# A new opening order, and twelve steps by halves in place of six, in a feature net in split fp32

## The chip, the cores and the metric

One core of a Trainium2 chip. The metric is the device time of the kernel in microseconds, the median of several runs. Engines: TensorE (PE in the profile; its weight loads are PEld), VectorE (DVE), ScalarE (ACT), GpSimd (POOL), SyncE (SP), which here issues nearly all loads.

## The reference

```python
# features (512, 2, 5128), W_ft (512, 5128), stm (512, 2, 1); r_features has 1024 rows of the batch
w = jnp.einsum('bpf,mf->bpm', features, W_ft) + b_ft
accumulator = stm * w
l1_x = jnp.clip(accumulator, 0.0, 1.0).reshape(features.shape[0], -1)
l2_x = jnp.clip(l1_x @ W1.T + b1, 0.0, 1.0)
return l2_x @ W2.T + b2
```

For a batch of 1024 and two perspectives nearly all of the work is one product in fp32: 512 outputs x 2048 columns over 5128 features. What follows (bias, scale by `stm`, clip, two small layers) is short.

## The kernel before

**The split.** A product in fp32 is made of three in fp32r: each operand is rounded to a `hi` part on ScalarE, VectorE takes the remainder `lo` = raw - `hi`, and TensorE adds `hi*hi`, `hi*lo` and `lo*hi`. The big product is also done by a two by two block scheme with seven block products in place of eight: features go in pairs of 128 rows (A, the first, and B, the second), outputs in two halves of 256 and columns in two halves of 1024. Three passes of 20 steps and a last one of 10 make `STEPS` = 70. A step takes one pair and adds two block products, a first half (`pos` 0) and a second (`pos` 1), each twelve products of 128x128 by 128x512: two row tiles by two column tiles by three splits.

**The steps of pass 0.** The first half of step g takes raw blocks as they are loaded: w block 0 and x block 0. I call it A of g. The second half needs sums: `sums_of(g)` on VectorE (lines 398 to 422) adds two w blocks (line 407, `w_sum`), subtracts two x blocks (line 417, `x_sum`) and keeps a further combination of w for later (line 421, `s_kept`). I call the second half B of g. So A needs loads, a rounding and a remainder; B needs loads, sums, a rounding and a remainder.

**Steps by halves and whole steps.** The first `OPEN` = 6 steps run by halves in the order `OPEN_HALVES`: A0 A1 B0 A2 B1 B2 A3 B3 A4 B4 A5 B5. ScalarE's `open_half` (290 to 315) rounds w, then x of one half, VectorE's `open_low` (380 to 396) takes their remainders (389 for w, 394 for x, 1024 columns), and TensorE's `open_products` (562 to 593) issues four `hi*hi`, four `lo` w by `hi` x, and four `hi` w by `lo` x, waiting for counts of `open_hi` and `open_lo` in turn. From step 6 on ScalarE's `round_step` (317) rounds both halves of w in one instruction (324) and of x in another (329, 2048 columns), VectorE's `low_step` (437) takes both remainders the same way (440, 443), and TensorE's `step` (595) waits once for each. The order on VectorE is written out by hand (476 to 492): in whole steps `sums_of(g + 1)` stands ahead of `low_step(g)`, and before the first of them `sums_of(6)` as well. At steps 13, 15, 16 and 17 VectorE also prepares the last eight feature rows (496, 502, 506).

**Buffers.** `HI` = 3 sets of rounded operands; a half of step g waits until step g - 3 is done (`step_done`, raised by the last product of B). `RAW` = 6 slots of raw blocks; the load of step g waits for step g - 6. The first `STAGED` = 3 steps load their A blocks to `open_x` and `open_w`, which lie in the room of `c_early`.

**Loads.** SP issues them in program order: w block 0 of step 0, its x block in two pieces of 512 columns, then for the halves of the staged steps in their order (221 to 228), then for steps 3 and on (229 to 252). A load of one x block is 512 KB, of one w block 128 KB; a whole step of pass 0 is 1.44 MB. ScalarE issues none. GpSimd waits for `step_done` 9 and then clears and loads the last rows' operands.

**Warm-up.** TensorE starts with `WARM_UP` = 16 products of 256 columns on zeros (680).

Of the kernel before, what the change touches and what calls it, by code (L numbers as in the profile page):

```python
# [24 lines left out]
ACT = mybir.ActivationFunctionType  # L25

P = 128
BANK = 512
WARM_UP = 16
K_PAIRS = 20  # L30
COLS = 1024
MH = 256
PASSES = 3
STEPS = PASSES * K_PAIRS + K_PAIRS // 2
STAGED = 3
OPEN = 6
RAW = 6
RAW_HOME = 4
HI = 3
OPEN_HALVES = ((0, 0), (1, 0), (0, 1), (2, 0), (1, 1), (2, 1), (3, 0), (3, 1), (4, 0), (4, 1), (5, 0), (5, 1))  # L40
TURN = 2 * K_PAIRS

HALVES = (((0, 0, 0), (1, 1, 4)), ((1, 1, 0), (0, 0, 4)), ((1, 0, 0), (0, 1, 4)), ((0, 0, 0), (1, 1, 0)))
# [7 lines left out]
def feature_net(nc, x_p, w_p, x_rest, w_rest, stm, b_ft, w1_t, b1, w2_t, b2, out):  # L51
# [10 lines left out]
    with ctx:  # L62
        base = (nc.sbuf_base + 63) // 64 * 64

        place = [base]
# [10 lines left out]
        def sem(name):  # L76
            return ctx.enter_context(nc.semaphore(name))
# [16 lines left out]
        c_at = place[0]  # L94
# [1 line left out]
        c_late = sb("c_late", [P, 2, 2 * COLS], at=xs_at + 4 * CST * COLS)  # L96
        c_all = [c_early[:, 0, :], c_early[:, 1, :], c_late[:, 0, :], c_late[:, 1, :]]
        open_x = sb("open_x", [P, STAGED, COLS], at=c_at)
        open_w = sb("open_w", [P, STAGED, MH], at=c_at + 4 * STAGED * COLS)
        xr_raw = sb("xr_raw", [P, COLS], at=c_at)  # L100
        wr_raw = sb("wr_raw", [P, 4, MH], at=c_at + 4 * COLS)
        xr = sb("xr", [P, COLS], F32R)
        wr = sb("wr", [P, 4, MH], F32R)

        stm_at = xs_at + 4 * (TST + 4) * COLS
# [20 lines left out]
        open_x_loaded = [sem(f"open_x_loaded{j}") for j in range(STAGED + 1)]  # L126
        open_hi = sem("open_hi")
        open_lo = sem("open_lo")
        x_sum = sem("x_sum")
        w_sum = sem("w_sum")  # L130
        s_kept = sem("s_kept")
# [83 lines left out]

        @block.sync
        def _(sp):
            sp.dma_start(open_w[:, 0, :], w_p[0, :, 0, :]).then_inc(open_w_loaded[0], 16)
            sp.dma_start(open_x[:, 0, 0:BANK], x_p[0, :, 0, 0:BANK]).then_inc(open_x_loaded[0], 16)
            sp.dma_start(open_x[:, 0, BANK:COLS], x_p[0, :, 0, BANK:COLS]).then_inc(open_x_loaded[STAGED], 16)  # L220
            for g, pos in OPEN_HALVES[1:2 * STAGED]:
                if pos == 0:
                    sp.dma_start(open_w[:, g, :], w_p[g, :, 0, :]).then_inc(open_w_loaded[g], 16)
                    sp.dma_start(open_x[:, g, :], x_p[g, :, 0, :]).then_inc(open_x_loaded[g], 16)
                else:
                    sp.dma_start(ws[:, raw_w(g) + 1, :], w_p[g, :, 1, :]).then_inc(w_loaded[g], 16)
                    sp.dma_start(ws[:, KEPT + g, :], w_p[g, :, 2, :]).then_inc(s_loaded[g], 16)
                    sp.dma_start(xs[:, TST + g, :], x_p[g, :, 1, :]).then_inc(t_loaded[g], 16)
            for g in range(STAGED, STEPS):
                f, k = pass_of(g)  # L230
                if g in (TURN + RAW_HOME, TURN + RAW_HOME + 1):
                    sp.wait_ge(x_sum, TURN + 2 * (g - TURN - RAW_HOME + 1))
                elif TURN <= g < TURN + RAW_HOME:
                    sp.wait_ge(step_done, g - RAW_HOME + 1)
                elif g >= RAW:
                    sp.wait_ge(step_done, g - RAW + 1)
                i, j, n = raw_w(g), raw_x(g), slot(g)
                if f == 0:
                    sp.dma_start(ws[:, i:i + 2, :], w_p[k, :, 0:2, :]).then_inc(w_loaded[n], 16)
                    sp.dma_start(ws[:, KEPT + k, :], w_p[k, :, 2, :]).then_inc(s_loaded[n], 16)  # L240
                    sp.dma_start(xs[:, j, :], x_p[k, :, 0, :]).then_inc(x_loaded[n], 16)
                    sp.dma_start(xs[:, TST + k, :], x_p[k, :, 1, :]).then_inc(t_loaded[n], 16)
                elif f == 1:
                    sp.dma_start(ws[:, i:i + 2, :], w_p[k, :, 0:2, :]).then_inc(w_loaded[n], 16)
                    sp.dma_start(xs[:, j:j + 2, :], x_p[k, :, 1:3, :]).then_inc(x_loaded[n], 16)
                elif f == 2:
                    sp.dma_start(ws[:, i:i + 2, :], w_p[k, :, 2:4, :]).then_inc(w_loaded[n], 16)
                    sp.dma_start(xs[:, j:j + 2, :], x_p[k, :, 2:4, :]).then_inc(x_loaded[n], 16)
                else:
                    for pos in range(2):  # L250
                        sp.dma_start(ws[:, i + pos, :], w_p[2 * k + pos, :, 3, :]).then_inc(w_loaded[n], 16)
                        sp.dma_start(xs[:, j + pos, :], x_p[2 * k + pos, :, 3, :]).then_inc(x_loaded[n], 16)
                if g == TURN + 10:
                    sp.wait_ge(x_sum, TURN + 6)
                    sp.dma_start(stm_all[:, :, :].rearrange("p h n -> p (h n)"),
                                 stm.rearrange("(a n) -> a n", a=1).broadcast_to([P, 2 * COLS]))\
                        .then_inc(stm_loaded, 16)
            for n, h in enumerate((1, 0)):
                sp.wait_ge(res_ready, n + 1)
                sp.dma_start(out.rearrange("(h q n) -> h q n", h=2, q=Q)[h], res[:, h, :]).then_inc(stored, 16)  # L260
            sp.wait_ge(stored, 32)
# [27 lines left out]
        def _(sc):  # L289
            def open_half(n, g, pos):  # L290
                if g >= HI:
                    sc.wait_ge(step_done, g - HI + 1)
                if pos == 0 and g < STAGED:
                    sc.wait_ge(open_w_loaded[g], 16)
                    nc.scalar.activation(w_hi[:, g, 0, :], open_w[:, g, :], ACT.Copy).then_inc(open_hi, 1)
                    sc.wait_ge(open_x_loaded[g], 16)
                    if g == 0:
                        nc.scalar.activation(x_hi[:, 0, 0, 0:BANK], open_x[:, 0, 0:BANK], ACT.Copy)\  # L298
# [2 lines left out]
                        nc.scalar.activation(x_hi[:, 0, 0, BANK:COLS], open_x[:, 0, BANK:COLS], ACT.Copy)\  # L301
                            .then_inc(open_hi, 1)
                    else:
                        nc.scalar.activation(x_hi[:, g, 0, :], open_x[:, g, :], ACT.Copy).then_inc(open_hi, 1)  # L304
                elif pos == 0:
                    sc.wait_ge(w_loaded[slot(g)], w_count(g))
                    nc.scalar.activation(w_hi[:, g % HI, 0, :], ws[:, raw_w(g), :], ACT.Copy).then_inc(open_hi, 1)
# [23 lines left out]
            def drain(f):  # L331
                for b in range(8):
# [16 lines left out]
                    else:  # L349
# [2 lines left out]
                        nc.scalar.activation(to, src, ACT.Identity, bias=b_ft_col[:, m:m + 1])\  # L352
                            .then_inc(drained, 1)

            for n, (g, pos) in enumerate(OPEN_HALVES):
                open_half(n, g, pos)
            for g in range(OPEN, STEPS):
# [21 lines left out]
        def _(dve):  # L379
# [93 lines left out]
                                        b2_col[:, 0:1], None, ALU.add).then_inc(res_ready, 1)  # L473

            nc.vector.memset(idle[:, :], 0.0).then_inc(idle_zeroed, 1)
            open_low(0, 0, 0)
            open_low(1, 1, 0)
            sums_of(0)
            open_low(2, 0, 1)
            open_low(3, 2, 0)  # L480
            sums_of(1)
            open_low(4, 1, 1)
            sums_of(2)
            open_low(5, 2, 1)
            for g in range(STAGED, OPEN):
                sums_of(g)
                open_low(2 * g, g, 0)
                open_low(2 * g + 1, g, 1)
            sums_of(OPEN)
            fourth = PASSES * K_PAIRS  # L490
            for g in range(OPEN, STEPS):
# [61 lines left out]
        def _(pe):  # L553
# [8 lines left out]
            def open_products(n, g, pos):  # L562
# [3 lines left out]
                if n == 0:  # L566
# [8 lines left out]
                    for c in range(PERSP):  # L575
                        pe.wait_ge(open_lo, 2 + c)
                        for m in range(2):
                            product(m * 2 + c, wh, xl, m, c, False)
                    return
                pe.wait_ge(open_hi, before + 2)  # L580
                for m in range(2):
# [7 lines left out]
                for m in range(2):  # L589
                    for c in range(PERSP):  # L590
                        mm = product(bank + m * 2 + c, wh, xl, m, c, False)
                if pos == 1:
                    mm.then_inc(step_done, 1)

            def step(g):
                f, k = pass_of(g)
# [156 lines left out]
```

## Time and profile before

| | |
|---|---|
| runs | 410.91, 411.74, 411.70 us, median 411.7 |
| the profiled execution | 409.96 us, its span 408.2 us |
| TensorE | 98% of the span busy, 1764 products |
| VectorE | 86%, 331 instructions |
| ScalarE | 47%, 182 instructions |
| HBM read | 96.08 MB, 235 GB/s over the span |

In the span's 40 slices TensorE is at nine tenths in nearly all, the first ones at 8, 9, 9, 9, 7; the transfer engines stand at 7, 9, 9, 9, 7 tenths there with 232, 400, 397, 399, 275 GB/s. The profile's times of products are modelled at their ends, so their pace is read from start to start. The views of use here are the timeline of the first 60 us, the chain of work that ended last, and the windows.

### The profile page before, as it was taken

The page shows a single profiled execution, that of the slowest core. Times are in us where ns is not written, and L with a number is a line of the kernel's source. Part 1 is how long each engine was busy: PE and PEld are TensorE (multiplying, and loading weights), DVE is VectorE, ACT ScalarE, POOL GpSimd, SP SyncE. Part 2 cuts the span into 40 slices and gives each one's busy share as a digit, 9 for nine tenths or more (in the row PEclk, how much of TensorE's full clock was granted, in tenths as well). Part 3 has the DMA queues.
Part 4 walks back from the last instruction along what each step waited for, and adds up shares of the span by engine and source line. Part 5 has one row for each costly group of instructions (what it writes and reads, how often), then busy time and mean ns, then how long its engine had stood idle before and what let it go on. Part 6 is the DMA issues. An engine that isn't in the chain of part 4 may idle for free.

```text
span 408.2 us, 4646 instructions
## 1 busy us (share of the span) xinstructions
PE 398.5 (98%) x1764; PEld 322.6 (79%) x1764; DVE 349.1 (86%) x331; ACT 191.4 (47%) x182; POOL 12.7 (3%) x32
## 2 busy tenths in 40 slices
PE   8999799999999999999999999999999999999995
PEld 5778688888888888888888888888888888888851
DVE  3999999899999999999984889999888755996335
ACT  4465644644474444444444854444444457444200
POOL 1000009000000000000000000000000000000000
PEclk9999999999999999999999999999999999999998
DMA  7999788987666777676506799876676777771000
GB/s 232 400 397 399 275 257 233 346 287 266 235 245 232 254 259 251 210 253 232 213 4 255 243 361 332 323 274 246 254 259 206 245 228 222 237 220 60 2 0 0
DMA packets 30182, 96.39 MB, mean 236 GB/s; under 512 B 3752, under 2 KB 9648, under 8 KB 24912
## 3 DMA queue, kind: packets, MB, share of 16 engines
q1 hardware_dynamic: 29536, 95.44, 67.7%
q0 software_dynamic: 624, 0.66, 0.8%
q8 instruction: 14, 0.23, 0.2%
q14 instruction: 8, 0.07, 0.0%
HBM read 96.08 MB, written 0.00 MB: 235 GB/s over the span
## 4 chain that ended last, share of the span: by engine, by line
PE 87%; DVE 7%; issue 2%; DMA 1%; ACT 1%; SPq 0%; DVEq 0%
PE sums L555 85%; DVE xs L417 2%; DMA open_x<-x_p 1%; DVE x_lo_home L394 1%; DVE x_lo_early L394 1%; ACT x_hi L315 1%; DVE ws L407 1%; PE sums L617 1%; PE sums L661 1%; DVE w_lo L389 1%; DVE x_lo_home L443 1%; DVE ws L421 0%; DVE c_early L536 0%; DVE c_early L540 0%; ACT x_hi L304 0%
## 5 line engine op out<-in xcount | busy, mean ns | idle before, releaser
L555 PE MATMUL sums<-x_hi,w_hi 128*128 128x512 f32 x560 | 175.0, 392 | 1.5 <-ACT x_hi L298 0.9
L555 PE MATMUL sums<-x_hi,w_lo 128*128 128x512 f32 x560 | 174.0, 391 | 0.0
L555 PEld LDWEIGHTS sums<-x_hi,w_hi 128*128 128x128 f32 x560 | 105.2, 189 | 26.2 <-ACT x_hi L315 1.4
L329 ACT ACTIVATE x_hi<-xs 128x2048 fp32r<-128x2048 f32 x64 | 122.1, 1908 | 3.9 <-DVE xs L434 3.0
L555 PEld LDWEIGHTS sums<-x_hi,w_lo 128*128 128x128 f32 x560 | 105.7, 189 | 22.2
L555 PE MATMUL sums<-x_lo_home,w_hi 128*128 128x512 f32 x384 | 119.1, 390 | 2.2 <-DVE x_lo_home L443 2.2
L324 ACT ACTIVATE w_hi<-ws 128x512 fp32r<-128x512 f32 x64 | 40.6, 635 | 169.4 <-PE sums L555 165.7
L443 DVE TENSOR_TENSOR x_lo_home<-xs,x_hi 128x2048 fp32r<-128x2048 f32 x44 | 100.6, 2287 | 6.7 <-ACT x_hi L329 6.6
L555 PEld LDWEIGHTS sums<-x_lo_home,w_hi 128*128 128x128 f32 x384 | 72.2, 188 | 17.7 <-issue 2.6
L440 DVE TENSOR_TENSOR w_lo<-ws,w_hi 128x512 fp32r<-128x512 f32 x64 | 43.9, 686 | 11.4 <-ACT w_hi L324 11.4
L427 DVE TENSOR_TENSOR xs<-xs 128x2048 f32<-128x2048 f32 x20 | 45.7, 2283 | 0.0
L434 DVE TENSOR_TENSOR xs<-xs 128x1024 f32<-128x1024 f32 x20 | 24.4, 1220 | 8.2 <-DMA xs<-x_p 8.2
L555 PE MATMUL sums<-x_lo_early,w_hi 128*128 128x512 f32 x96 | 28.9, 389 | 0.0
L443 DVE TENSOR_TENSOR x_lo_late<-xs,x_hi 128x2048 fp32r<-128x2048 f32 x10 | 22.9, 2287 | 3.8 <-ACT x_hi L329 3.8
L555 PE MATMUL sums<-x_lo_late,w_hi 128*128 128x512 f32 x80 | 25.3, 389 | 0.0
L443 DVE TENSOR_TENSOR x_lo_early<-xs,x_hi 128x2048 fp32r<-128x2048 f32 x10 | 22.9, 2285 | 0.0
L555 PEld LDWEIGHTS sums<-x_lo_early,w_hi 128*128 128x128 f32 x96 | 18.0, 188 | 3.8
L417 DVE TENSOR_TENSOR xs<-xs 128x1024 f32<-128x1024 f32 x17 | 20.8, 1222 | 0.0
L555 PEld LDWEIGHTS sums<-x_lo_late,w_hi 128*128 128x128 f32 x80 | 15.0, 188 | 3.0
L536 DVE SCALAR_TENSOR_TENSOR c_early<-sums,b_ft_col,c_early 128x512 f32<-128x512 f32 x4 | 3.0, 749 | 11.3 <-PE sums L647 11.3
L375 ACT ACTIVATE part<-sums,b_col 128x512 f32<-128x512 f32 x2 | 1.4, 687 | 21.9 <-PE sums L701 11.6
L431 DVE TENSOR_TENSOR ws<-ws 128x256 f32<-128x256 f32 x20 | 8.4, 419 | 3.2 <-DMA ws<-w_p 3.2
(74 smaller groups left out, 150.7 us busy)
## 6 DMA issues: line engine op xcount, KB each, us to landing
xs<-x_p SPq DMA_DIRECT2D x40, 1024.0 KB, 5.6
xs<-x_p SPq DMA_DIRECT2D x57, 512.0 KB, 6.7
ws<-w_p SPq DMA_DIRECT2D x57, 256.0 KB, 3.5
ws<-w_p SPq DMA_DIRECT2D x43, 128.0 KB, 4.6
open_x<-x_p SPq DMA_DIRECT2D x2, 512.0 KB, 6.6
stm_all<-stm SPq DMA_DIRECT2D x1, 1024.0 KB, 8.3
open_x<-x_p SPq DMA_DIRECT2D x2, 256.0 KB, 4.0
open_w<-w_p SPq DMA_DIRECT2D x3, 128.0 KB, 4.4
```

Of the source, the lines that this page charges most:

```text
L315: nc.scalar.activation(x_hi[:, g % HI, 1, :], xs[:, TST + g, :], ACT.Copy).then_inc(open_hi, 1)
L324: nc.scalar.activation(w_hi[:, g % HI, :, :], w_pair(g), ACT.Copy).then_inc(w_hi_ready, 1)
L329: nc.scalar.activation(x_hi[:, g % HI, :, :], x_pair(g), ACT.Copy).then_inc(x_hi_ready, 1)
L389: nc.vector.tensor_tensor(w_lo[:, slot(g), pos, :], w_src, w_hi[:, g % HI, pos, :].bitcast(F32), ALU.subtract).then_inc(open_lo, 1)
L394: nc.vector.tensor_tensor(low_x(g)[:, pos, a:b], x_src[:, a:b], x_hi[:, g % HI, pos, a:b].bitcast(F32), ALU.subtract)\
L417: nc.vector.tensor_tensor(xs[:, TST + k, :], xs[:, TST + k, :], b11, ALU.subtract)\
L427: nc.vector.tensor_tensor(x_pair(g), xs[:, j + 1:j + 2, :].broadcast_to([P, 2, COLS]), x_pair(g), ALU.subtract).then_inc(x_sum, 1)
L431: nc.vector.tensor_tensor(ws[:, i + 1, :], ws[:, i + 1, :], ws[:, KEPT + k, :], ALU.subtract)\
L434: nc.vector.tensor_tensor(xs[:, j + 1, :], xs[:, j + 1, :], xs[:, TST + k, :], ALU.subtract)\
L440: nc.vector.tensor_tensor(w_lo[:, slot(g), :, :], w_pair(g), w_hi[:, g % HI, :, :].bitcast(F32), ALU.subtract).then_inc(w_lo_ready, 1)
L443: nc.vector.tensor_tensor(low_x(g), x_pair(g), x_hi[:, g % HI, :, :].bitcast(F32), ALU.subtract).then_inc(x_lo_ready, 1)
L555: return nc.tensor.matmul(sums[:, bank, :], w[:, m * P:(m + 1) * P], x[:, c * BANK:(c + 1) * BANK], start=start, stop=stop, skip_group_che ...
```

## The change

The opening order becomes A0 A1 A2 B0 A3 B1 B2 B3, followed by A4 B4 up to A11 B11: twelve steps by halves (`OPEN` = 12). Four steps are staged; `open_w` moves to the room of `xr`, so that four x blocks fit in that of `c_early`. The loads on SP follow the new order. The w blocks of steps 0 and 1 are issued by ScalarE at its start. VectorE takes the sums of steps 0 to 3 just ahead of the remainders of their B, and those of steps 4 to 11 ahead of the remainders of their A. A new semaphore `a_done` is raised by the last product of each A in the opening; ScalarE's rounding for A of step g waits for it in place of `step_done`. The warm-up has 22 products in place of 16.

```diff
-WARM_UP = 16
+WARM_UP = 22
-STAGED = 3
-OPEN = 6
+STAGED = 4
+OPEN = 12
-OPEN_HALVES = ((0, 0), (1, 0), (0, 1), (2, 0), (1, 1), (2, 1), (3, 0), (3, 1), (4, 0), (4, 1), (5, 0), (5, 1))
+OPEN_HALVES = ((0, 0), (1, 0), (2, 0), (0, 1), (3, 0), (1, 1), (2, 1), (3, 1)) + tuple(
+    (g, pos) for g in range(STAGED, OPEN) for pos in range(2))
...
-        open_w = sb("open_w", [P, STAGED, MH], at=c_at + 4 * STAGED * COLS)
+        xr_at = place[0]
         xr = sb("xr", [P, COLS], F32R)
+        open_w = sb("open_w", [P, STAGED, MH], at=xr_at)
...
         def _(sp):
-            sp.dma_start(open_w[:, 0, :], w_p[0, :, 0, :]).then_inc(open_w_loaded[0], 16)
             sp.dma_start(open_x[:, 0, 0:BANK], x_p[0, :, 0, 0:BANK]).then_inc(open_x_loaded[0], 16)
...
                 if pos == 0:
-                    sp.dma_start(open_w[:, g, :], w_p[g, :, 0, :]).then_inc(open_w_loaded[g], 16)
+                    if g > 1:
+                        sp.dma_start(open_w[:, g, :], w_p[g, :, 0, :]).then_inc(open_w_loaded[g], 16)
                     sp.dma_start(open_x[:, g, :], x_p[g, :, 0, :]).then_inc(open_x_loaded[g], 16)
...
             def open_half(n, g, pos):
                 if g >= HI:
-                    sc.wait_ge(step_done, g - HI + 1)
+                    sc.wait_ge(step_done if pos else a_done, g - HI + 1)
...
+            for g in range(2):
+                sc.dma_start(open_w[:, g, :], w_p[g, :, 0, :]).then_inc(open_w_loaded[g], 16)
             for n, (g, pos) in enumerate(OPEN_HALVES):
                 open_half(n, g, pos)
...
-            open_low(0, 0, 0)
-            open_low(1, 1, 0)
-            sums_of(0)
-            open_low(2, 0, 1)
-            open_low(3, 2, 0)
-            sums_of(1)
-            open_low(4, 1, 1)
-            sums_of(2)
-            open_low(5, 2, 1)
-            for g in range(STAGED, OPEN):
-                sums_of(g)
-                open_low(2 * g, g, 0)
-                open_low(2 * g + 1, g, 1)
+            for n, (g, pos) in enumerate(OPEN_HALVES):
+                if pos if g < STAGED else not pos:
+                    sums_of(g)
+                open_low(n, g, pos)
             sums_of(OPEN)
...
-                if pos == 1:
-                    mm.then_inc(step_done, 1)
+                mm.then_inc(step_done if pos else a_done, 1)
```

## Rows read from the trace of the kernel before

**Rows 1.** The page of the profile: span; busy time, share and instructions of each engine.
```profile
span 408.2 us, 4646 instructions
...
PE 398.5 (98%) x1764; PEld 322.6 (79%) x1764; DVE 349.1 (86%) x331; ACT 191.4 (47%) x182; POOL 12.7 (3%) x32
```

**Rows 2.** The chain of work that ended last: start, duration (us), what.
```profile
44.45 182.53 PE sums L555 x804
...
226.97 0.23 PE sums L617
```

**Rows 3.** Timeline of TensorE in the opening: start, duration (us), engine, line, operation [idle before].
```profile
1.06 3.60 PE L680 MATMUL sums<-idle 128*128 128x256 bf16 x16 [1.06 <-DVE idle L475]
...
5.51 2.43 PE L555 MATMUL sums<-x_hi,w_hi 128*128 128x512 f32 x4 [0.85 <-ACT x_hi L298]
...
7.74 1.91 PE L555 MATMUL sums<-x_hi,w_lo 128*128 128x512 f32 x4
...
10.44 1.08 PE L555 MATMUL sums<-x_hi,w_hi 128*128 128x512 f32 x4
...
22.43 1.21 PE L555 MATMUL sums<-x_hi,w_hi 128*128 128x512 f32 x4 [0.62 <-ACT x_hi L315]
...
30.77 1.07 PE L555 MATMUL sums<-x_hi,w_hi 128*128 128x512 f32 x4
...
41.65 0.61 PE L555 MATMUL sums<-x_hi,w_hi 128*128 128x512 f32 x2
...
44.45 0.70 PE L555 MATMUL sums<-x_lo_home,w_hi 128*128 128x512 f32 x2 [2.18 <-DVE x_lo_home L443]
```

**Rows 4.** Timeline of VectorE and ScalarE in the opening, columns as in rows 3.
```profile
10.93 1.23 DVE L417 TENSOR_TENSOR xs<-xs,open_x 128x1024 f32<-128x1024 f32 x1
...
12.19 1.06 ACT L315 ACTIVATE x_hi<-xs 128x1024 fp32r<-128x1024 f32 x1 [0.76 <-DVE xs L417]
...
13.28 1.23 DVE L394 TENSOR_TENSOR x_lo_home<-xs,x_hi 128x1024 fp32r<-128x1024 f32 x1 [0.46 <-ACT x_hi L315]
...
14.76 1.22 DVE L394 TENSOR_TENSOR x_lo_home<-open_x,x_hi 128x1024 fp32r<-128x1024 f32 x1
...
15.90 0.42 DVE L407 TENSOR_TENSOR ws<-ws 128x256 f32<-128x256 f32 x1
...
19.72 0.42 DVE L407 TENSOR_TENSOR ws<-ws 128x256 f32<-128x256 f32 x1
...
28.29 0.42 DVE L407 TENSOR_TENSOR ws<-ws 128x256 f32<-128x256 f32 x1
...
37.79 0.43 DVE L407 TENSOR_TENSOR ws<-ws 128x256 f32<-128x256 f32 x1
...
42.01 2.29 DVE L443 TENSOR_TENSOR x_lo_home<-xs,x_hi 128x2048 fp32r<-128x2048 f32 x1
```

**Rows 5.** Timeline: issues of line 224, their landing times, and the first one's reader.
```profile
2.61 0.43 SPq L224 DMA_DIRECT2D open_x<-x_p  x1
...
5.10 0.97 SPq L224 DMA_DIRECT2D open_x<-x_p  x1
...
8.32 1.06 ACT L304 ACTIVATE x_hi<-open_x 128x1024 fp32r<-128x1024 f32 x1 [1.31 <-DMA open_x<-x_p]
...
DMA to landing us min/median/max: 5.7/6.6/7.5
```

**Rows 6.** Windows: stretch, length, busy (count) per engine, PE clock, DMA share, GB/s.
```profile
5.50:9.50 4.00, 3.99 (x9) 2.71 (x10) 1.80 (x4) 2.03 (x3) 0.00 (x0) 1.00 0.93 299
9.50:13.30 3.80, 3.80 (x17) 2.82 (x15) 3.34 (x6) 1.53 (x3) 0.00 (x0) 1.00 1.03 397
```

**Rows 7.** Timeline of VectorE behind the opening: steps 12, 13 and 39.
```profile
69.67 2.29 DVE L443 TENSOR_TENSOR x_lo_home<-xs,x_hi 128x2048 fp32r<-128x2048 f32 x1
...
74.81 0.43 DVE L496 TENSOR_TENSOR wr_raw<-wr_raw 128x256 f32<-128x256 f32 x1 [1.04 <-DMA wr_raw<-w_rest]
...
220.22 2.28 DVE L443 TENSOR_TENSOR x_lo_home<-xs,x_hi 128x2048 fp32r<-128x2048 f32 x1
```

More of the change, by code:

```diff
@@ L128, in feature_net @@
         open_lo = sem("open_lo")
+        a_done = sem("a_done")
         x_sum = sem("x_sum")
@@ L291, in open_half @@
                 if g >= HI:
-                    sc.wait_ge(step_done, g - HI + 1)
+                    sc.wait_ge(step_done if pos else a_done, g - HI + 1)
                 if pos == 0 and g < STAGED:
                     sc.wait_ge(open_w_loaded[g], 16)
-                    nc.scalar.activation(w_hi[:, g, 0, :], open_w[:, g, :], ACT.Copy).then_inc(open_hi, 1)
+                    nc.scalar.activation(w_hi[:, g % HI, 0, :], open_w[:, g, :], ACT.Copy).then_inc(open_hi, 1)
                     sc.wait_ge(open_x_loaded[g], 16)
@@ L303, in open_half @@
                     else:
-                        nc.scalar.activation(x_hi[:, g, 0, :], open_x[:, g, :], ACT.Copy).then_inc(open_hi, 1)
+                        nc.scalar.activation(x_hi[:, g % HI, 0, :], open_x[:, g, :], ACT.Copy).then_inc(open_hi, 1)
                 elif pos == 0:
@@ L577, in open_products @@
                         for m in range(2):
-                            product(m * 2 + c, wh, xl, m, c, False)
+                            mm = product(m * 2 + c, wh, xl, m, c, False)
+                    mm.then_inc(a_done, 1)
                     return
```

## The prediction

> **What bounds the kernel now.** Read the page first, then the chain, then the opening on the timeline. The page gives TensorE 398.5 us busy of 408.2 and VectorE 349.1 [rows 1]: the products are the bound if they never wait. The chain shows where that holds: from 44.45 us to the layers at the end it is products alone, 182.53 us in its first unbroken piece [rows 2]. So the whole question is how early TensorE can run without a gap, and the only place to look is what lies before 44.45 us.
>
> The opening has twelve products to each half step. Steps by halves run unbroken from 30.77 to 41.65, four half steps in 10.88 us: 2.72 us for a half, 5.44 for a step, 0.227 for a product [rows 3]. Between the first real product at 5.51 and 44.45 lie 146 products, 33.1 us at that pace, so 5.8 us are lost. One piece of it is 2.35 us (44.45, less 41.65 and its two products of 0.45): step 6, the first that is not by halves, waits for its `x_lo`, and VectorE is the releaser [rows 3]. A smaller piece, an idle time of 0.62, stands before 22.43; the rest lies in the first products, up to 13.3.
>
> Behind these waits is one chain on VectorE and ScalarE. I call T the start of the first sum of x (10.93 in this trace) [rows 4]. From T the rounded x of B0 is ready 2.35 us later (10.93 to 13.28, by way of ScalarE at 12.19). The `sums_of` of step 1 starts at T+4.97 (15.90); in between lie B0's remainders and one first half's. A second half with its sums and nothing in between takes 3.82 us (15.90 to 19.72), because VectorE waits for ScalarE's rounding inside it. The products of B2 start 2.71 us behind their sums (19.72 to 22.43). Once a first half's remainders lie between the sums and the second half's, the wait is gone: steps 4 and 5 take 9.50 us together (28.29 to 37.79), 4.75 a step [rows 4]. There VectorE gains 5.44 - 4.75 = 0.69 us a step on TensorE. The change to whole steps then takes 6.66 us from the sums of step 6 to the first product with its remainders (37.79 to 44.45) [rows 3, 4]: `sums_of(7)` comes first, and the remainder of x is one piece of 2.29 us.
>
> **Twelve steps by halves.** In the new order B3's sums are the last that carry the wait, so B3 takes the part that B2 has now, and steps 4 to 11 run at 4.75. The transition comes after eight such steps and not after three. Now it is 2.35 us late; five more steps at 0.69 make 3.45, so it would be 1.1 us early, and the stall goes. No product is added. On the engines each further step costs two more instructions on VectorE and on ScalarE, and stays below the 5.44 us of TensorE. With `a_done` a first half waits only for its own buffer of three steps before; ahead of it on ScalarE nothing else then queues, and VectorE reaches A11 nine microseconds behind A8's last product, so that wait is free.
>
> What is late next? At step 12 today VectorE is done at 71.96 [rows 7], and TensorE, which starts step 12 at 44.00 + 6 x 5.44 = 76.6, wants it at 77.1: 5.1 us in hand. After the change it is done at T+60.95 (sums of step 4 at T+16.43, eight steps of 4.75, 6.52 to the end of the piece), and is wanted at T+62.2 (below): 1.1 us with the 0.14 from its end to the product. Behind it lies step 13, where VectorE now waits 1.04 us for weights of the last rows [rows 7]; they are loaded after `step_done` 9, so they come earlier with TensorE and that wait goes, which leaves 2.8 us less in hand than now from there on. Today step 13 has 4.5 us in hand (line 496 at 74.81 and 3.2 us more to its remainder of x, against 82.5), and that is the smallest up to step 20, so 1.7 remain. The smallest of all, 1.3 us before step 39 (220.22 + 2.28 against 226.97 less fourteen products) [rows 2, 7], hangs on loads that wait for `step_done` and moves along. I cost all this at nothing; without the cover each microsecond short is one lost.
>
> **The opening order.** Here the change gives back some. A2 now goes ahead of B0, so T depends on x of step 2: its landing, then 1.09 us to round it (12.19 to 13.28), 1.14 for its remainder (14.76 to 15.90), and 0.36 for the sum of w before the sum of x (2.71 less 2.35) [rows 4]: T = landing + 2.59. It lands at 12.6 now (5.10 + 7.5) and x of step 1 at 8.3 (2.61 + 5.7) [rows 5]. In the new order 1.97 MB are asked for up to it, against 1.31 up to x of step 1 (both orders) and 2.75 now. The 0.66 MB between take 1.65 us at 397 GB/s and 2.2 at 299 [rows 6]: 9.95 to 10.5, and up to 0.5 earlier if the head start below carries through. I take 10.2 and so T = 12.8, with 12.2 and 13.7 as ends (9.6 and 11.1). The sum of x of step 0 also needs its own load, which has 2.75 MB up to it, as x of step 2 has now: 12.6, just inside.
>
> Then by the same intervals: sums of step 1 at T+4.97 (A3 fills the place that A2 has now), of step 2 at T+8.79, of step 3 at T+12.61; B3's products at T+15.32; A4's one half later, with the 0.18 us that a restart costs (22.43 to 30.77 is 8.34 us, three halves 8.16): T+18.2. That is 31.0 against 30.77 now [rows 3]. The remainder of A4's x is due eight products later, at T+20.0, and ready at T+19.85, the same 0.2 us to spare as A3 has now. So the order by itself costs 0.25 us: one first half of VectorE's work and 1.65 us of loads more in front, one chained half fewer behind.
>
> **W loads on ScalarE's queue.** An issue takes 0.43 us on SP [rows 5]; taking two W loads off puts x of step 0 some 0.43 us ahead and later loads 0.9. ScalarE issues them ahead of its first rounding. If its table load went first, W0 would land later by that load; up to 5.3, TensorE's end of warming up less a rounding or so, nobody would miss it. What it is worth: nothing on the sum beyond the head start in T's range, since by the time of x of step 1 the transfer engines are busy at 0.93 [rows 6]. The Trainium skill (Trainium Kernel Development and Optimization, Key Constraints) says the same of queues in general: several issuing engines share the same 16 DMA engines and save only the issue time. By that rule alone the sum stays 0.25 us late; had a second queue brought bandwidth of its own, T would be early.
>
> **22 warm-up products.** Sixteen take 3.60 us from 1.06 and TensorE then idles 0.85; six more at 0.225 end near 6.0, so the first real product is up to 0.5 us later. The first real products run at the lower clock: at 7.74 four take 1.91 us where at 10.44 they take 1.08 [rows 3]. The row of the clock prints 1.00 there [rows 6], but 0.43 us for 512 columns is 1.2 GHz and 0.227 the 2.4 level. Neither is on the path: TensorE has to be through seven halves by T+15.3 = 28.1, 6.0 + 19.0 = 25.0 at the higher level, so 3.1 us of slow products are hidden, about fifteen of them at 0.2 more each, and the trace has at most twelve. If the clock rose later than that, it would cost, where now the wait at 42 us would swallow it.
>
> **Sum.** The third product of step 6 starts at 44.45 now and at T + 18.2 + 10.88 + 0.45 = 42.3 after: 2.1 us, which is 2.35 less 0.25. The profiled execution took 409.96 (span 408.2), so 407.9; it lies 1.74 below the median of the timed runs, 411.7, and I carry the difference over: **409.6 us**. With T's ends, 409.0 to 410.5.
>
> **Rivals.** (1) *The loads were held back by their issue.* Then x of step 2, issued at 2.6 and not 5.1, lands by 9.3, T is below 12, and the gain is 3 us or more: 408.6. For it, the shares below 1 before 9.5 us; against, they are 0.93 already [rows 6]. (2) *The gain is hidden or halved.* x of step 2 lands after 11.5 because both queues' small pieces interleave ahead of it, or the second queue costs something outside the span, which no row here bounds: 1 to 2 us of the gain go, 410.6 to 411.6. (3) *Slower: the halves stay coupled.* If in steps 4 to 11 VectorE waited for ScalarE in each second half as it does at 13.28 [rows 4], a step would take 3.82 + 1.47 = 5.29 us and gain only 0.15. Eight steps bring the transition to T+65.4, 3.2 us late, 0.85 more than now; with the 0.25 that is 412.8. It turns from gain to loss where a step passes 5.15 us. Against it stand the two steps of 4.75. (4) *The change doesn't act*, because step 12 stalls as step 6 did: that needs VectorE 3.4 us behind the count above, and would give 411.9; I put it with (2).
>
> **How the numbers follow.** Forecast 0.60, rival 1 0.10, rivals 2 and 4 together 0.23, rival 3 0.07. A measurement of this kernel can tell about 0.2%, 0.8 us, from no change. Forecast and rival 1 lie beyond that, and 0.04 of rival 2 does (410.6 to 410.9); 0.18 of it lies within, 0.01 beyond on the other side. Faster 0.74, same 0.18, slower 0.08. The range leaves out rival 3, the far half of rival 1 and the last of rival 2: 408.4 to 411.3.
>
> **What would show it.** In the profile after: the first sum of x near 12.8 (right between 12.2 and 13.7); the sums of steps 1 to 4 behind it at 4.97 and then 3.82 each; A4's products near 31.0; 4.75 a step to step 11; no idle time of TensorE between 31 us and the end; VectorE's wait at line 496 gone. Wrong would be: a wait of TensorE for `x_lo` near 74.5, a T before 12 or after 14, or a gain that the span shows and the whole time does not.

## The result

| | before | after |
|---|---|---|
| median, five runs each | 411.01 us (409.88 to 411.74) | 407.06 us (406.20 to 407.74) |
| the profiled execution, its span | 409.96, 408.2 | 406.20, 404.4 |
| the same comparison in a later session | 410.90 (17 runs) | 406.58 (4 runs) |

The ratio is 0.9907 with a 95% interval of 0.9883 to 0.9930: 4.0 us faster, 3.8 us by the two profiles. The forecast was 409.6 with a range of 408.4 to 411.3. The direction was right; the time lies below the range.

The page of the profile after, its span and its engines, against [rows 1]:

```profile
span 404.4 us, 4671 instructions
...
PE 397.4 (98%) x1770; PEld 322.7 (80%) x1770; DVE 349.9 (87%) x343; ACT 193.4 (48%) x194; POOL 12.8 (3%) x32
```

The timeline of VectorE, ScalarE and TensorE in the opening, against [rows 3, 4] (start, duration in us, engine, line, operation, idle time before it). Lines 412 and 422 are 407 and 417 of before, 307 is 304, 318 is 315, 551 is 555, 448 is 443. In every kernel below, T is the start of the first row `xs<-xs,open_x`.

```profile
8.96 1.06 ACT L307 ACTIVATE x_hi<-open_x 128x1024 fp32r<-128x1024 f32 x1 [0.50 <-DMA open_x<-x_p]
...
11.53 1.22 DVE L422 TENSOR_TENSOR xs<-xs,open_x 128x1024 f32<-128x1024 f32 x1
...
16.50 0.42 DVE L412 TENSOR_TENSOR ws<-ws 128x256 f32<-128x256 f32 x1
...
20.32 0.42 DVE L412 TENSOR_TENSOR ws<-ws 128x256 f32<-128x256 f32 x1
...
23.02 1.19 PE L551 MATMUL sums<-x_hi,w_hi 128*128 128x512 f32 x4 [0.26 <-ACT x_hi L318]
...
24.14 0.42 DVE L412 TENSOR_TENSOR ws<-ws 128x256 f32<-128x256 f32 x1
...
26.84 1.20 PE L551 MATMUL sums<-x_hi,w_hi 128*128 128x512 f32 x4 [0.80 <-ACT x_hi L318]
...
27.96 0.42 DVE L412 TENSOR_TENSOR ws<-ws 128x256 f32<-128x256 f32 x1
...
29.69 1.07 PE L551 MATMUL sums<-x_hi,w_hi 128*128 128x512 f32 x4
```

T, the first sum of x, is at 11.53. Behind it everything stands where the count put it: the sums of step 1 at T+4.97, of step 2 at T+8.79, of step 3 at T+12.61, of step 4 at T+16.43, B2's products at T+11.49, B3's at T+15.31, A4's at T+18.16. Only T itself is 1.3 us earlier than the 12.8 that was taken; a T below 12 is one of the signs of being wrong that the prediction names.

Step 12, the first whole step, and step 13:

```profile
70.17 2.29 DVE L448 TENSOR_TENSOR x_lo_home<-xs,x_hi 128x2048 fp32r<-128x2048 f32 x1
...
73.21 0.62 PE L551 MATMUL sums<-x_hi,w_hi 128*128 128x512 f32 x2
...
73.67 0.61 PE L551 MATMUL sums<-x_lo_home,w_hi 128*128 128x512 f32 x2
...
74.18 0.42 DVE L492 TENSOR_TENSOR wr_raw<-wr_raw 128x256 f32<-128x256 f32 x1
```

The remainder of x is ready at 72.46 and wanted at 73.67: 1.2 us in hand, where 1.1 were worked out. At step 13 it is 1.7, as worked out (remainder of x ready at 77.40, wanted at 79.11). TensorE goes on at 73.67 with no idle time, and line 492 (496 of before) waits for nothing. The chain of work that ended last shows the same as one unbroken piece from B3 on, against [rows 2] where it starts at 44.45:

```profile
26.84 196.59 PE sums L551 x866
```

### The profile page after: what moved, and what is told of

Its sections match the earlier page's. It is cut to its first block, busy times and chain, and to the rows that moved or that the text cites. A ratio compares the mean times of both kernels' runs of the same rounds, so it can differ in the third digit from the quotient of the medians.

```text
span 404.4 us, 4671 instructions
## 1 busy us (share of the span) xinstructions
PE 397.4 (98%) x1770; PEld 322.7 (80%) x1770; DVE 349.9 (87%) x343; ACT 193.4 (48%) x194; POOL 12.8 (3%) x32
## 4 chain that ended last, share of the span: by engine, by line
PE 92%; DVE 3%; DMA 2%; ACT 1%; issue 1%; SPq 0%; DVEq 0%
PE sums L551 89%; DMA open_x<-x_p 2%; DVE xs L422 1%; ACT x_hi L318 1%; PE sums L613 1%; PE sums L657 1%; DVE x_lo_home L399 1%; DVE ws L412 0%; DVE c_early L532 0%; DVE c_early L536 0%; ACT x_hi L307 0%; PE sums L697 0%; DVE c_early L540 0%; PE sums L665 0%; PE sums L671 0%
## 5 line engine op out<-in xcount | busy, mean ns | idle before, releaser
L551 PE MATMUL sums<-x_hi,w_hi 128*128 128x512 f32 x560 | 172.3, 391 | 1.1 <-ACT x_hi L318 1.1
L551 PE MATMUL sums<-x_hi,w_lo 128*128 128x512 f32 x560 | 171.1, 389 | 0.0
L332 ACT ACTIVATE x_hi<-xs 128x2048 fp32r<-128x2048 f32 x58 | 110.7, 1909 | 5.0 <-DVE xs L439 3.2
L327 ACT ACTIVATE w_hi<-ws 128x512 fp32r<-128x512 f32 x58 | 36.8, 635 | 151.0 <-PE sums L551 148.4
L448 DVE TENSOR_TENSOR x_lo_home<-xs,x_hi 128x2048 fp32r<-128x2048 f32 x40 | 91.5, 2286 | 6.8 <-ACT x_hi L332 6.8
L445 DVE TENSOR_TENSOR w_lo<-ws,w_hi 128x512 fp32r<-128x512 f32 x58 | 39.8, 686 | 11.2 <-ACT w_hi L327 11.0
L448 DVE TENSOR_TENSOR x_lo_early<-xs,x_hi 128x2048 fp32r<-128x2048 f32 x8 | 18.3, 2283 | 0.0
L318 ACT ACTIVATE x_hi<-xs 128x1024 fp32r<-128x1024 f32 x12 | 12.8, 1063 | 8.1 <-DVE xs L422 8.1
L399 DVE TENSOR_TENSOR x_lo_home<-xs,x_hi 128x1024 fp32r<-128x1024 f32 x12 | 14.6, 1220 | 1.8 <-ACT x_hi L318 1.8
L315 ACT ACTIVATE w_hi<-ws 128x256 fp32r<-128x256 f32 x12 | 5.0, 418 | 16.7 <-DVE ws L412 16.7
```

The source lines that it names most:

```text
L315: nc.scalar.activation(w_hi[:, g % HI, 1, :], ws[:, raw_w(g) + 1, :], ACT.Copy)\
L318: nc.scalar.activation(x_hi[:, g % HI, 1, :], xs[:, TST + g, :], ACT.Copy).then_inc(open_hi, 1)
L327: nc.scalar.activation(w_hi[:, g % HI, :, :], w_pair(g), ACT.Copy).then_inc(w_hi_ready, 1)
L332: nc.scalar.activation(x_hi[:, g % HI, :, :], x_pair(g), ACT.Copy).then_inc(x_hi_ready, 1)
L399: nc.vector.tensor_tensor(low_x(g)[:, pos, a:b], x_src[:, a:b], x_hi[:, g % HI, pos, a:b].bitcast(F32), ALU.subtract)\
L445: nc.vector.tensor_tensor(w_lo[:, slot(g), :, :], w_pair(g), w_hi[:, g % HI, :, :].bitcast(F32), ALU.subtract).then_inc(w_lo_ready, 1)
```

## The experiments

Times are medians with their lowest and highest run; the kernel before, run beside them, had 410.19 (19 runs), 410.97 (8), 410.90 (17) and 410.74 (8) in the four groups. The groups ran on different chips, so the ratio in the last column compares better than the bare times. T is read from one profile each.

| kernel | time, us | T | against before beside it |
|---|---|---|---|
| before, twelve by halves | 407.81 (406.90 to 407.93) | 11.36 | 0.9917 (0.9890 to 0.9943) |
| before, wait filled | 409.87 (409.04 to 410.48) | 10.86 | 0.9979 (0.9964 to 0.9993) |
| before, W on ScalarE | 410.47 (408.48 to 411.77) | 10.27 | 0.9992 (0.9973 to 1.0012) |
| after, six by halves | 411.25 (409.73 to 412.71) | 11.65 | 1.0013 (0.9994 to 1.0032) |
| after, ten by halves | 406.63 (406.37 to 407.25) | 12.16 | 0.9897 (0.9869 to 0.9925) |
| after, W on SP | 407.82 (407.51 to 408.17) | 13.47 | 0.9930 (0.9906 to 0.9953) |
| after, padded issues | 407.93 (one run) | 13.14 | |
| after, SP held back | 407.18 (406.55 to 407.49) | 12.55 | 0.9915 (0.9885 to 0.9945) |
| after, old order | 406.40 (406.18 to 406.55) | 9.87 | 0.9889 (0.9862 to 0.9916) |
| after, 16 warm-up products | 406.52 (406.44 to 406.67) | 11.60 | 0.9898 (0.9870 to 0.9925) |
| after, again | 406.58 (406.47 to 407.19) | 12.18 | 0.9900 (0.9870 to 0.9931) |
| further version | 405.57 (405.19 to 405.82) | 9.97 | 0.9876 (0.9849 to 0.9903) |

### The halves: six, ten, twelve

The kernel before with one size changed (and the list of halves carried on to match):

```diff
-OPEN = 6
+OPEN = 12
```

> The kernel before with OPEN = 12 and nothing else: same opening order, loads and warm-up. Theory: T stays at 10.9, the wait of 2.2 us at step 6 goes and none takes its place at step 12, because VectorE gains 0.69 us in each of nine such steps; that gives 2.4 us, and in those runs where the clock fell behind the wait (granted clock 0.5 for 3.4 us, worth 1.7 us) it gives that too. So the profile is 407.5 us and the median 2.5 to 3.4 us below that of the kernel before, and the spread of its runs is under 1 us. Rival (the stall moves to step 12, or the clock's fall has another cause): the gain is under 1.5 us, or the runs spread over 1.5 us as those of before do.

It gained 3.2 us by the medians, 3.4 by the ratio. Its profile, at 407.9, is 0.4 above the expected, as T is: the span is 406.1, 2.1 us below 408.2 although T came 0.4 us later in it, and its chain has TensorE unbroken from B2 on:

```profile
22.84 202.10 PE sums L556 x890
```

So this one edit holds most of the gain. The reverse, the kernel after with six:

```diff
-OPEN = 12
+OPEN = 6
```

> The changed kernel with six steps by halves in place of twelve, all else as changed. Theory: VectorE gains 0.69 us a step on TensorE in steps 4 and 5 only, and at the transition to whole steps it is needed at T+29.5 while it is ready at T+32.6: TensorE waits 3.1 us before the third product of step 6, and the time is 3.1 us longer than the changed kernel's, 410.2. Rival (the halves of themselves bring nothing, the gain is in the order and the loads): within 0.8 us of the changed kernel.

```profile
41.23 0.70 PE L551 MATMUL sums<-x_hi,w_hi 128*128 128x512 f32 x2 [0.35 <-ACT x_hi L332]
...
44.22 0.70 PE L551 MATMUL sums<-x_lo_home,w_hi 128*128 128x512 f32 x2 [2.29 <-DVE x_lo_home L448]
```

The third product of step 6 starts at 44.22, 3.2 us later than the 41.0 at which it stands after (29.69 and 50 products), as expected: 2.29 of idle time before it and 0.35 before the step. The time was expected at 410.2 and is 411.25. It is 4.2 us above the kernel after and 4.7 above the one with 16 warm-up products beside it, a microsecond or more beyond the waits. The clock, below, can be part of that; no run splits it. And with ten:

```diff
-OPEN = 12
+OPEN = 10
```

> The changed kernel with ten steps by halves. Theory: VectorE's gain of 0.69 us a step leaves it 1.1 us early at a transition after twelve steps, so after ten it is 0.3 us late: TensorE waits 0.2 to 0.5 us at the third product of step 10, the time is 0.2 to 0.6 us above that of twelve, and so short a wait brings no fall of the clock. Rival (the reserve at step 12 is larger than worked out, or the pace is not 0.69): no wait at step 10, or one of over 1 us.

```profile
61.29 2.29 DVE L448 TENSOR_TENSOR x_lo_early<-xs,x_hi 128x2048 fp32r<-128x2048 f32 x1
...
62.97 0.61 PE L551 MATMUL sums<-x_hi,w_hi 128*128 128x512 f32 x2
...
63.73 0.70 PE L551 MATMUL sums<-x_lo_early,w_hi 128*128 128x512 f32 x2
```

The remainder of x ends at 63.58 and the third product starts at 63.73 instead of 63.42: 0.3 us late, the figure expected. With 3.2 late at six and 1.2 early at twelve that makes 0.7 us a step throughout. The time was expected 0.2 to 0.6 us above that of twelve, and the median is no higher; 0.3 us in an opening whose T varies by 0.6 can't be seen in it.

### The clock behind the wait

```diff
-            sp.dma_start(open_w[:, 0, :], w_p[0, :, 0, :]).then_inc(open_w_loaded[0], 16)
...
-                    sp.dma_start(open_w[:, g, :], w_p[g, :, 0, :]).then_inc(open_w_loaded[g], 16)
+                    if g > 1:
+                        sp.dma_start(open_w[:, g, :], w_p[g, :, 0, :]).then_inc(open_w_loaded[g], 16)
...
+            for g in range(2):
+                sc.dma_start(open_w[:, g, :], w_p[g, :, 0, :]).then_inc(open_w_loaded[g], 16)
```

> The kernel before with only its first two W loads moved to ScalarE's queue. Theory (the second queue makes the early loads land sooner): x of step 1 lands near 7.1 and not 8.3, the first sum of x starts 0.8 to 1.2 us earlier than 10.93, and since that chain runs on to the transition at 44.45, the time is 0.8 to 1.2 us shorter, about 410.0. Rival (nothing): the first sum stays at 10.9 and the time is 411.0.

T moved to 10.27, 0.7 us earlier where 0.8 to 1.2 were expected, and the third product of step 6 with it, from 44.45 to 43.75. Yet the profile's span grew from 408.2 to 408.9 and the median did not follow: the expected gain in time did not come. Its fastest run, 408.48, does lie 1.2 us below the fastest of before beside it, 409.69. TensorE's timeline, the piece of the chain behind the wait and the windows around it (stretch, length, busy and count of PE, PEld, DVE, ACT, POOL, clock, DMA share, GB/s) say where the 0.7 us went, and more:

```profile
10.27 1.22 DVE L419 TENSOR_TENSOR xs<-xs,open_x 128x1024 f32<-128x1024 f32 x1
...
43.75 0.70 PE L557 MATMUL sums<-x_lo_home,w_hi 128*128 128x512 f32 x2 [2.19 <-DVE x_lo_home L445]
...
45.51 1.05 PE L557 MATMUL sums<-x_lo_home,w_hi 128*128 128x512 f32 x2
...
46.36 1.05 PE L557 MATMUL sums<-x_hi,w_lo 128*128 128x512 f32 x2
...
48.62 0.63 PE L557 MATMUL sums<-x_hi,w_lo 128*128 128x512 f32 x2
```

```profile
43.75 184.12 PE sums L557 x804
```

```profile
43.70:45.10 1.40, 1.35 (x6) 1.11 (x7) 1.40 (x3) 0.63 (x1) 0.00 (x0) 0.91 1.09 356
...
45.10:48.50 3.40, 3.40 (x10) 2.69 (x9) 3.40 (x5) 1.91 (x1) 0.00 (x0) 0.53 0.67 250
...
48.50:52.00 3.50, 3.50 (x17) 2.89 (x16) 3.50 (x5) 1.34 (x2) 0.00 (x0) 1.00 0.07 19
```

A good microsecond behind the idle stretch, with TensorE already at work again, the granted clock fell to the lower of its two levels, 1.2 GHz, and stayed there for 3.4 us. Two products go from 0.45 us to 0.85 (45.51 to 46.36) until 48.62. That cost 1.6 us: the same 804 products take 184.12 us here and 182.53 in before [rows 2], where the clock did not fall. So the kernel before pays for its wait in every run and, if its slower runs are of this kind, for the clock in some. That was tested by keeping TensorE busy and changing nothing else:

```diff
+FILL = 14
...
+                        if n == 0 and m == 0 and g == OPEN:
+                            for _ in range(FILL):
+                                nc.tensor.matmul(sums[:, 7, 0:BANK // 2], idle[:, 0:P], idle[:, :],
+                                                 start=False, stop=False, skip_group_check=True)
```

> The kernel before with fourteen products of zeros (256 columns of bf16, added to a bank) put into the wait of TensorE at step 6; they change no sum and end before the wait does. Theory: the wait costs its 2.2 us in every run, and in about every third run of the kernel before 1.7 us more, because the clock falls behind the idle stretch (granted clock 0.5 for 3.4 us); with TensorE kept busy the wait stays at 44 us but the clock no longer falls, so no run lies above 410.8 and the median falls by 0 to 1 us, to about 410.0. Rival (the slower third of the runs has another cause): runs of 411.2 and more appear as often as in the kernel before.

```profile
42.01 1.70 PE L629 MATMUL sums<-idle 128*128 128x256 bf16 x14
...
44.36 0.70 PE L556 MATMUL sums<-x_lo_home,w_hi 128*128 128x512 f32 x2 [0.65 <-DVE x_lo_home L444]
```

The third product starts at 44.36, 0.1 us earlier than before, as T does, and the idle stretch is down from 2.18 to 0.65 us. None of twelve runs is above 410.48, where nine of the seventeen runs of before beside them are at 410.90 or more. The median falls by 1.0 us, the ratio's interval (0.9964 to 0.9993) leaves out no change. That is as expected.

The mean granted clock that is on record for every run says the same. Of the 52 runs of before beside the experiments, the 13 with a mean of 0.993 or less took 411.01 us or more, and the 15 with 0.997 or more took 410.78 or less. The 24 in between lie anywhere from 409.75 to 412.13. A mean near 0.996 can't tell a fall behind the wait from one in the last microseconds, which costs little: the profile of before has 0.997 from a fall at 405 us alone. With the wait filled no mean is below 0.994; with twelve halves in the kernel before one of five is 0.993, and it has the second lowest time.

The Trainium skill (TensorE: Matmul & The Clock Gate, Part 1) has it that the slow level is the rest state and activity lifts it. The rows agree on the rise: it came at 48.3 us, under unbroken products. That a fall can come a microsecond into the work, and in some executions only, is what these rows add.

### The early loads

```diff
+            sp.dma_start(open_w[:, 0, :], w_p[0, :, 0, :]).then_inc(open_w_loaded[0], 16)
...
-                    if g > 1:
-                        sp.dma_start(open_w[:, g, :], w_p[g, :, 0, :]).then_inc(open_w_loaded[g], 16)
+                    sp.dma_start(open_w[:, g, :], w_p[g, :, 0, :]).then_inc(open_w_loaded[g], 16)
...
-            for g in range(2):
-                sc.dma_start(open_w[:, g, :], w_p[g, :, 0, :]).then_inc(open_w_loaded[g], 16)
```

> The changed kernel with the first two W loads back on SP, W0 first and W1 just ahead of x of step 1; all else as changed. Theory (the second queue makes the early loads land sooner, and T, the start of the first sum of x, follows them): T goes from 11.53 back toward 12.8, every interval behind T stays (sums of step 1 at T+4.97, products of A4 at T+18.2), and the whole gets 1.0 to 1.3 us longer, about 408.2. Rival (the order of the transfers or luck made them early, the queue does nothing): T stays within 0.3 us of 11.5, and the time is the same as the changed kernel's.

The windows of the kernel after, then of this one:

```profile
5.50:9.50 4.00, 4.00 (x18) 3.02 (x16) 3.03 (x5) 2.85 (x6) 0.00 (x0) 1.00 1.01 374
```

```profile
5.50:9.50 4.00, 3.51 (x15) 2.35 (x12) 1.54 (x3) 1.13 (x3) 0.00 (x0) 1.00 0.91 305
...
10.90 1.06 ACT L307 ACTIVATE x_hi<-open_x 128x1024 fp32r<-128x1024 f32 x1 [0.23 <-DMA open_x<-x_p]
...
13.47 1.22 DVE L420 TENSOR_TENSOR xs<-xs,open_x 128x1024 f32<-128x1024 f32 x1
```

x of step 2 is rounded at 10.90 instead of 8.96, T is 1.9 us later and the span 2.0 us longer. The medians show less: 407.82 against 407.06 after and 406.52 with 16 warm-up products beside it, 0.8 to 1.3 us. The two kernels move the same bytes up to there; at 5.5 to 9.5 us one moves them at 374 GB/s and the other at 305. Two causes are possible, the second queue or the earlier issue on the first. Padding SP with two tiny loads where W0 and W1 had stood leaves the second queue and takes the earlier issue away:

```diff
+            sp.dma_start(spare[0:16, 0:8], w_p[0, 0:16, 0, 0:8]).then_inc(spare_loaded, 16)
             sp.dma_start(open_x[:, 0, 0:BANK], x_p[0, :, 0, 0:BANK]).then_inc(open_x_loaded[0], 16)
...
+                    if g == 1:
+                        sp.dma_start(spare[0:16, 8:16], w_p[0, 0:16, 0, 8:16]).then_inc(spare_loaded, 16)
```

> The changed kernel with two tiny extra loads (16 rows of 32 bytes, not used by anything) on SP in the places where W0 and W1 were issued before; W0 and W1 stay on ScalarE. So SP issues every load as late as in the kernel with the W loads on SP, but the large transfers still have two queues. Issue theory: x of step 2 lands late because SP issues it late, T goes from 11.5 to 12.5 or more. Queue theory: the second queue is what speeds the early transfers, T stays below 12.1 (0.5 us for the first issue at most).

```profile
2.57 0.42 SPq L232 DMA_DIRECT2D open_x<-x_p  x1
...
10.57 1.06 ACT L312 ACTIVATE x_hi<-open_x 128x1024 fp32r<-128x1024 f32 x1 [0.27 <-DMA open_x<-x_p]
...
13.14 1.22 DVE L427 TENSOR_TENSOR xs<-xs,open_x 128x1024 f32<-128x1024 f32 x1
```

SP issues x of step 1 at 2.57 here, and T went to 13.14 with both queues in use, so the second queue as such makes 0.3 us between these two profiles, which is within the scatter of T. But the tiny loads may cost transfer time of their own. The next kernel adds none and only starts SP later:

```diff
+            sp.wait_ge(add_up_built, 2)
             sp.dma_start(open_x[:, 0, 0:BANK], x_p[0, :, 0, 0:BANK]).then_inc(open_x_loaded[0], 16)
```

> The changed kernel with SP held back at its start until GpSimd's first two small instructions are done (about 1.4 us instead of 0.74), so that every load on SP is issued some 0.7 us later; no transfer is added, W0 and W1 stay on ScalarE's queue and go out in time. Issue theory: x of step 2 lands later by the whole delay or more, T is 12.3 to 13.2 (against 11.5 to 12.2), and the time is 0.7 to 1.2 us above the changed kernel's, 407.5 to 408.2. Transfer theory (the 16 transfer engines are the bound of the first 10 us, and what the extra small loads cost in the padded kernel was their own transfer time): T moves by 0.3 us or less.

```profile
1.33 0.41 SPq L222 DMA_DIRECT2D open_x<-x_p  x1
...
9.97 1.06 ACT L308 ACTIVATE x_hi<-open_x 128x1024 fp32r<-128x1024 f32 x1 [0.27 <-DMA open_x<-x_p]
...
12.55 1.22 DVE L423 TENSOR_TENSOR xs<-xs,open_x 128x1024 f32<-128x1024 f32 x1
```

SP starts 0.59 us later and T is 12.55, against 11.53, 11.60, 11.65, 12.16 and 12.18 in the five profiles with W on ScalarE and SP on time, 11.8 in the mean: 0.7 us, the delay about one for one. The time was expected at 407.5 to 408.2 and is 407.18; only 0.1 to 0.7 us of the delay shows in it. T lies 0.4 us above the latest of the five, so the issue on SP is a true term, though one profile can't say more than that it counts about one for one. W on SP delays x of step 2 by 0.9 us of issue and T by 1.6 against that mean; what makes up the rest was not found.

### The order and the warm-up

```diff
-OPEN_HALVES = ((0, 0), (1, 0), (2, 0), (0, 1), (3, 0), (1, 1), (2, 1), (3, 1)) + tuple(
+OPEN_HALVES = ((0, 0), (1, 0), (0, 1), (2, 0), (1, 1), (2, 1), (3, 0), (3, 1)) + tuple(
```

> The changed kernel with the old opening order A0 A1 B0 A2 B1 B2 A3 B3 (loads with it), W0 and W1 on ScalarE's queue, 22 warm-up products and OPEN = 12 kept. Theory: T is near 10.3 as in the kernel before with its W loads on ScalarE, and the products of A4 start at T+19.8 = 30.1 against 29.7 in the changed kernel, so the order by itself is worth 0.4 us and the time is 0.2 to 0.6 us above the changed kernel's. Rival (the order is where the gain comes from): over 1 us above it.

```profile
9.87 1.22 DVE L422 TENSOR_TENSOR xs<-xs,open_x 128x1024 f32<-128x1024 f32 x1
...
21.35 1.20 PE L551 MATMUL sums<-x_hi,w_hi 128*128 128x512 f32 x4 [0.66 <-ACT x_hi L318]
...
29.64 1.07 PE L551 MATMUL sums<-x_hi,w_hi 128*128 128x512 f32 x4
```

T is 9.87, B2 starts at T+11.48 and A4 at T+19.8 = 29.64, the interval expected, at the very time at which the new order has it (29.69). T was expected at 10.3, A4 at 30.1 and the time 0.2 to 0.6 us above that of the changed kernel. The median is 0.2 us below those of the kernel with ten halves beside it and of the changed kernel run again. The new order brings nothing and costs nothing that can be measured.

```diff
-WARM_UP = 22
+WARM_UP = 16
```

> The changed kernel with 16 warm-up products in place of 22. Theory: TensorE's early products are hidden behind the chain of the sums, so with more of them at the lower clock level the products of B3 still start at T+15.3 and the time stays the same within 0.5 us, 407.0. Rival (the clock level is part of the gain): the first twelve or more products take 0.43 us each, B2 and B3 come later than their rounded x, and the time grows by 1 us or more.

406.52: no different. The warm-up is hidden, as the chain of the sums said.

### The changed kernel again, and a further version

> The changed kernel once more, on the same chip as the two beside it. Theory: 406.3 to 407.7, no run spread beyond that, with T between 11.4 and 12.3, since x of step 2 lands between 8.9 and 9.7 in all profiles in which W0 and W1 are on ScalarE's queue. Rival (the first profile was a lucky one): T of 12.8.

```profile
9.61 1.06 ACT L307 ACTIVATE x_hi<-open_x 128x1024 fp32r<-128x1024 f32 x1 [1.22 <-DMA open_x<-x_p]
...
12.18 1.22 DVE L422 TENSOR_TENSOR xs<-xs,open_x 128x1024 f32<-128x1024 f32 x1
```

T was 12.18, at the end of what was expected, and the time 406.58. x of step 2 lands at 8.9 in one profile and at 9.6 in the other with the same program, so T is known to some 0.6 us and no better.

With the chain known, its remaining waits can be taken out: the old order with A3 ahead of B2, and the sums of steps 1 and 2 ahead of the remainders of A2 and A3.

```diff
+OPEN_HALVES = ((0, 0), (1, 0), (0, 1), (2, 0), (1, 1), (3, 0), (2, 1), (3, 1)) + tuple(
...
+SUMS = {(0, 1): 0, (2, 0): 1, (3, 0): 2, (3, 1): 3, **{(g, 0): g for g in range(STAGED, OPEN)}}
...
-                if pos if g < STAGED else not pos:
-                    sums_of(g)
+                if (g, pos) in SUMS:
+                    sums_of(SUMS[g, pos])
```

> A further version: the changed kernel with the order A0 A1 B0 A2 B1 A3 B2 B3, loads alike, and on VectorE the sums of step 1 ahead of A2's remainders and those of step 2 ahead of A3's, so that only B0 and B3 keep the wait for ScalarE's rounding inside. Theory: T near 9.9 as in the old order, sums of step 2 at T+8.2, of step 3 at T+13.0, of step 4 at T+16.8 = 26.7, so the products of A4 start near 28.6 against 29.7, no gap of TensorE from A2 on, and 0.9 to 1.2 us less than the changed kernel. Rival (the loads of step 1's sums land later than VectorE wants them, or B0's products wait): gain under 0.4 us.

```profile
12.33 210.23 PE sums L552 x926
...
28.83 1.07 PE L552 MATMUL sums<-x_hi,w_hi 128*128 128x512 f32 x4
```

405.57, 1.0 us below the changed kernel beside it (406.58). TensorE is unbroken from B0 at 12.33 on, and A4 starts at 28.83, 0.9 us earlier than after; 28.6 and 0.9 to 1.2 us were expected. It beats both kernels.

## Why the prediction was off, step by step

**What bounds the kernel, and the chain behind T: right.** All intervals from T to A4 came out within 0.05 us in the profile after, and again in the experiments that keep its order (B3's products at T+15.29 with W on SP, T+15.30 with SP held back). The bound before was this chain and the wait at step 6, as read. Two terms beside it were mis-sized, the loads and the clock; together they put the time below the range.

**Twelve steps by halves: right.** 2.35 us was the wait's own size, and 0.69 us a step, 1.1 us in hand at step 12 (measured 1.2), 1.7 at step 13 and 0.3 us short at ten all came out. One small thing was left out: the restart behind the wait costs 0.1 us more. Rival 3, coupled halves, is refuted by the same rows: the sums of steps 4 to 12 are 4.75 us apart. Rival 4, a stall at step 12, is refuted by the remainder that was ready in time. Rival 2 needed x of step 2 to land after 11.5; it was rounded at 8.96.

**W loads on ScalarE's queue: the first step that failed.** The prediction said this is worth nothing on the sum beyond the head start in T's range, since the transfer engines are busy at 0.93. A share of 0.93 was read as a full engine. After the change the same stretch has a share of 1.01 and carries 374 GB/s instead of 299. T is 11.5 to 12.2, below the range of 12.2 to 13.7, and undoing the edit brings 13.5. This term was mis-sized: T 12.8 against 11.53 in the profile, 1.3 us of gain too little. It is the forecast's rival 1, loads held back by their issue, which had a chance of 0.10. The Trainium skill (Trainium Kernel Development and Optimization, Key Constraints) says that a second issuing queue saves only issue time. The padded kernel agrees, since it kept the second queue and lost the gain. The mistake was to count the issue time of the first loads as at most half a microsecond: 0.93 us of it moved T by 1.6. Why T moved by more than the issue is not shown.

**The opening order: right in size, wrong in place.** A cost of 0.25 us was worked out from T; with both orders on the same loads the difference is 0.2 us or less. T itself is 1.7 us earlier in the old order (9.87 against 11.60), which the longer way to A4 takes back.

**The clock: a missing term, and the second step that failed.** The sum was made on a profile in which the clock did not fall behind the wait, and 1.74 us, the distance of that execution from the median of three runs, was carried over as a constant. It was no constant, and three runs were few: the median of five is 411.01, 1.05 above the profile. Filling the wait without shortening it took 1.0 us off the median, and removing the wait in the kernel before took 3.2 to 3.4 us off, where wait and restart are 2.45. In the changed kernel the profile and the median are 0.9 us apart. That the loads alone don't explain the miss is seen with W on SP: T is 13.47 there, for which the sum gives 410.3 (409.6 and the 0.67 by which T is past 12.8), and the time was 407.82. The prediction saw that a late rise of the clock at the start is hidden, and did not ask what an idle stretch of 2.2 us does to the clock behind it.

**The account.** Wait and restart 2.45, A4 earlier by 1.08 in the profile, together 3.5 of the 3.76 us between the two profiles. The other 0.2 lies in the last two products, which in before ran after the granted clock had fallen (0.75 from 405 to 406 us, then 0.50). The chain of before, then of after:

```profile
405.54 0.60 PE sums L675 x2
```

```profile
401.99 0.40 PE sums L671 x2
```

In the medians the clock behind the wait adds about 1, and T, which was early in this profile, takes some 0.3 back: about 4.5 worked out, 4.0 and 4.3 measured. Against the forecast, 409.6 less 407.06 is 2.54 us: T 1.27, the carried-over difference 0.88 (1.74 against 0.86), the last products 0.2, the restart 0.1, and under 0.1 that is not placed. With T alone right the sum would have given 408.3, with the carried-over difference alone right 408.7; the range ends at 408.4, and the measured time is below both.

## What to carry to other kernels

Count a chain from a named event (here T) and check the event and the intervals apart: the intervals were exact, and the event, a landing, was where the error lay. A transfer share a little below one in the first microseconds doesn't mean that issuing earlier is worthless; so the load that the chain hangs on should be issued first, and loads that stand ahead of it in its queue moved off. An idle stretch of the matmul engine costs its length in every run and can cost a fall of the clock behind it in some. Here a wait of 2.2 us in mid-kernel was worth about a microsecond more than it said, and the spread of the runs is where that was seen.

## What the runs showed of the hardware

An idle stretch of 2.19 us on TensorE was followed, some 1.1 us after its end, by 3.4 us at a granted clock of 0.50 (1.2 GHz; 0.53 over the window shown), and stretches of 2.18 and 2.29 us in the profiles of two other kernels, before and after with six halves, were not. With 14 short products of zeros in it (idle 0.65) no run showed the longer time. Waits of 0.3 to 0.8 us in the kernels after had no such sequel in their profiles.

From 5.5 to 9.5 us the loads moved at 271 to 305 GB/s in the four profiles with W on SP (299 in before [rows 6]), at 336 with it on ScalarE in the kernel before, and at 354 to 401 with it on ScalarE in the kernel after and its variants. The share of the transfer engines hardly tells these apart: 0.91 to 0.96 in the first group, 0.95 to 1.04 in the others. The padded kernel, late in its issues, has 310 (share 0.91). The one with SP held back has 355, no lower than the changed kernel run again (354), so what sets the rate is not shown.
